# The bias of the values: one load and GpSimd adds instead of an accumulating DMA, in a two-layer graph network kernel

## The reference

```python
def setup_inputs(...):      # x is 4096 x 512, adj 4096 x 4096, sparse and symmetric, biases are small
...
def _L0_gnn_ref(x, spatial_encoding, edge_encoding, Wq, bq, Wk, bk, Wv, bv):
    q = x @ Wq.T + bq
    k = x @ Wk.T + bk
    v = x @ Wv.T + bv
    scale = 1.0 / jnp.sqrt(jnp.asarray(q.shape[-1], q.dtype))
    a = q @ k.T * scale + spatial_encoding + edge_encoding
    attn = jax.nn.softmax(a, axis=-1)
    return attn @ v
...
# --- layer 0 (adj_resnorm) ---
x = _layernorm(x + _L0_gnn_ref(x, adj, adj, ...), axis=-1)
# --- layer 1 (adj_resnorm) ---
x = _layernorm(x + _L1_gnn_ref(x, adj, W, b, a_self, a_neigh), axis=-1)
```

## Time and profile before

| | us |
|---|---|
| median of 3 runs | 1680.17 (1675.47 to 1684.64) |
| the profiled execution | 1676.71 |
| its span in the profile | 1674.9 |
| TensorE (PE) busy | 1561.0, 93% |
| VectorE (DVE) busy | 1218.4, 73% |
| GpSimd (POOL) busy | 866.4, 52% |
| ScalarE (ACT) busy | 539.9, 32% |
| mean transfer rate | 241 GB/s |

### The profile page before, as it was taken

How to read it: one execution, slowest core, us unless ns; L and a number is a source line. 1 busy time by engine, 2 the same in 40 slices (tenths; PEclk the granted TensorE clock), 3 DMA queues, 4 the chain that set the end, 5 groups by cost and what they waited for, 6 DMA issues and landing times.

```text
span 1674.9 us, 27914 instructions
## 1 busy us (share of the span) xinstructions
PE 1561.0 (93%) x10052; PEld 969.0 (58%) x10052; DVE 1218.4 (73%) x2438; ACT 539.9 (32%) x822; POOL 866.4 (52%) x809
## 2 busy tenths in 40 slices
PE   8999998999999999999999999999999999989830
PEld 3444587666666666666666666666666666644310
DVE  5798687688867876688768876887587867847335
ACT  4555401222232223222322233223322232246336
POOL 2987401556454644454545554555455545667343
PEclk9999999999999999999999999999999999999975
DMA  7467886679757886798669866896589667756347
GB/s 263 164 239 274 300 295 215 226 245 282 264 183 250 297 278 189 231 305 264 205 214 318 282 212 199 298 288 229 186 275 324 228 191 241 235 200 221 89 141 292
DMA packets 192396, 403.24 MB, mean 241 GB/s; under 512 B 20736, under 2 KB 26880, under 8 KB 191104
## 3 DMA queue, kind: packets, MB, share of 16 engines
q1 hardware_dynamic: 182912, 376.25, 67.0%
q0 software_dynamic: 9344, 25.17, 5.8%
HBM read 343.67 MB, written 57.67 MB: 240 GB/s over the span
## 4 chain that ended last, share of the span: by engine, by line
PE 83%; DVE 6%; DMA 4%; issue 2%; POOL 2%; ACT 1%; SPq 1%; another core or an unknown queue 0%; DVEq 0%; POOLq 0%; ACTq 0%
PE O L845 34%; PE S L804 30%; PE O L759 6%; PE X L759 5%; DMA yb<-y_scratch 3%; PE S L759 3%; PE O L804 2%; PE BC L759 1%; PE X L888 1%; POOL work L719 1%; DVE work L1362 1%; DVE ring L1601 1%; POOL ring L741 1%; DVE xr L1388 1%; DVE ring L1404 1%
## 5 line engine op out<-in xcount | busy, mean ns | idle before, releaser
L845 PE MATMUL O<-vring,ring 128*128 128x512 f16 x2928 | 707.5, 379 | 5.2 <-POOL ring L709 3.4
L804 PE MATMUL S<-yb,big 128*128 128x256 f16 x4974 | 621.3, 273 | 15.1 <-DMA yb<-y_scratch 6.9
L709 POOL TENSOR_TENSOR ring<-work,ring 128x512 f16<-128x512 f32 x236 | 282.6, 1198 | 599.5 <-ACT ring L1020 599.5
L804 PEld LDWEIGHTS S<-yb,big 128*128 128x128 f16 x4974 | 483.0, 98 | 167.4 <-issue 10.4
L845 PEld LDWEIGHTS O<-vring,ring 128*128 128x128 f16 x2928 | 286.1, 98 | 262.3 <-issue 7.4
L1141 ACT ACTIVATE work<-ring 128x512 f32<-128x512 f32 x256 | 160.8, 628 | 750.5 <-DVE ring L1327 705.9
L1336 DVE TENSOR_TENSOR ring<-S,ring 128x256 f32<-128x256 f32 x476 | 199.6, 419 | 219.6 <-PE S L804 216.9
L719 POOL TENSOR_TENSOR work<-work 128x512 f32<-128x512 f32 x248 | 342.9, 1383 | 7.0 <-ACT work L1141 5.9
L1362 DVE TENSOR_TENSOR work<-work,ring 128x512 f32<-128x512 f32 x248 | 207.4, 836 | 0.6
L1341 DVE TENSOR_TENSOR ring<-S,ring 128x256 f32<-128x256 f32 x357 | 150.6, 422 | 62.8 <-PE S L804 47.5
L1327 DVE TENSOR_TENSOR ring<-BC,ring 128x512 f32<-128x512 f32 x256 | 173.6, 679 | 1.8 <-PE BC L873 1.8
(11 more groups left out here) (145 smaller groups left out, 1096.3 us busy)
## 6 DMA issues: line engine op xcount, KB each, us to landing
ring<-in_adjT SPq DMA_DIRECT2D x256, 256.0 KB, 5.0
big<-in_adj SPq DMA_DIRECT2D x256, 256.0 KB
big<-x_scratch SPq DMA_DIRECT2D x126, 512.0 KB, 5.2
vring<-v_scratch SPq DMA_DIRECT2D x244, 256.0 KB
yb<-y_scratch SPq DMA_DIRECT2D x56, 256.0 KB, 6.2
y_scratch<-yb SPq DMA_DIRECT2D x7, 1792.0 KB, 10.6
ring<-in_xT SPq DMA_DIRECT2D x8, 1024.0 KB, 6.7
v_scratch<-vring SPq DMA_DIRECT2D x32, 256.0 KB, 2.6
```

Source lines behind the costliest of these rows:

```text
L709: pool.tensor_tensor(ring16[:, e % SLOTS, 1, :], pf[:, e % NPF, :], ring16[:, e % SLOTS, 0, :], ALU.subtract).then_inc(lo_done, 1)
L804: mm = pe.matmul(bank, keys_of(p, keys, a, c), yb[:, b % 2, queries, m, c, :], start=(start and c + a + m == 0), stop=(c == 1 and a == 1), ...
L845: mm = pe.matmul(O[j][:, :], ring16[:, e % SLOTS, a, j * P:(j + 1) * P], values_of(e)[:, m, :], start=(k + a + m == 0), stop=(k == NT - 1 ...
```

## The change

bv is loaded once a block by SP, as a fifth load behind the four of x, into `bvb`, which is the place of `x1h`. GpSimd adds it to the four tiles of `xr` with four instructions, two at r = 13 and two at r = 14, where it started one DMA before. The eviction of tile j waits for j + 1 of these adds.

```diff
+        bvb = work[:, 2560:3072]
...
-        xr_in, xb_in = sem("xr_in"), sem("xb_in")
+        xr_in, xb_set = sem("xr_in"), sem("xb_set")
...
                         sp.dma_start(xr[:, j, :], x[t * P:(t + 1) * P, :]).then_inc(xr_in, 16)
+                    sp.dma_start(bvb, row_of(bv)).then_inc(xr_in, 16)
...
-                if r == 13 and 1 <= b <= NB:
-
-                    pool.wait_ge(xr_in, b * JB * 16)
-                    pool.dma_start(xr[:, :, :], bv.rearrange("(a o n) -> a o n", a=1, o=1).broadcast_to([P, JB, D]),
-                                   accum_op=ALU.add).then_inc(xb_in, 16)
+                if r in (13, 14) and 1 <= b <= NB:
+
+                    pool.wait_ge(xr_in, b * (JB + 1) * 16)
+                    for j in (0, 1) if r == 13 else (2, 3):
+                        pool.tensor_tensor(xr[:, j, :], xr[:, j, :], bvb, ALU.add).then_inc(xb_set, 1)
...
-                dve.wait_ge(xb_in, (b + 1) * 16)
+                dve.wait_ge(xb_set, b * JB + j + 1)
```

## The result

The changed kernel takes 1695.07 us in the median of 5 runs (1691.64 to 1697.75), against 1680.17 before. The ratio is 1.0099, with a 95% interval of 1.0074 to 1.0123: slower by 1.0%. The forecast was 1676.7 us, the range 1670 to 1687. It was wrong, and on the other side.

What follows compares the result with a forecast made beforehand. TensorE, busy 1561.0 of 1674.9 us, was taken as the bound, losing time at block turns. -7.5 (DMA) + 0.7 (adds against VectorE) + 3.3 (tail) = -3.5 us, so 1676.7 us against the median 1680.2; range 1670 to 1687.

Steps and rivals of the forecast that it cites:

- The accumulating DMA: Turns between blocks: removing it frees DMA capacity, so the last piece of queries lands in time; -7.5 us.
- Rival 1: Turns between blocks: the queries stay late and only 1.7 us comes back; +2.3 us in all, 1682.5 us; chance 0.13.
- GpSimd's own time: Mid-kernel, r = 13 and 14: slack and idle time cover the adds; 0, or 25 us without that cover.
- the fifth load in mid-kernel: SP at r = 11: it moves the loads behind it by about 0.5 us, on chunks that aren't late; 0.
- the wait before the eviction: VectorE at r = 1 of the next block: it asks for xb_set some 30 us later; 0.
- So an add can hold a maximum back by up to 0.92 us: Mid-kernel, 28 adds against VectorE's running maximum: between 0 and 26 us, taken as 0.1 us a block, 0.7 us.
- the reads that TensorE waits for stand in front of the maximum: Mid-kernel, VectorE: why a maximum of 1.50 us delayed TensorE by nothing, its step still taking 9.76 us.
- Rival 2: Mid-kernel, r = 13 and 14: adds hold VectorE back, 11.2 us in place of 0.7; +7.0 us, 1687.2 us; chance 0.14.
- The tail: Last block, x loads to row sums: later landing and adds delay the running sums; +3.3 us, bounds 2.1 to 6.2.
- the fifth load adds one issue, 0.44 us: Tail: the load of bv lengthens GpSimd's wait for the last block's x rows by one issue, 1.75/4 = 0.44 us.
- The adds, 1.16 + 2.54 - 0.8 = 2.9 us: Tail: two adds replace the 1.38 us command, two more come two sums later, and 0.8 us is taken back.
- rival 3: Tail: after a longer gap TensorE's 36 products run at a lower clock, costing 3.4 us; -0.1 in all, 1680.1 us; chance 0.15.

Runs made afterwards that it cites:

- load_only: The changed kernel with bv loaded but not added, so the output lacks the bias; ratio 0.9960 to the kernel before.
- one_by_one: The changed kernel with one add behind each running sum of r = 13 and 14, not two behind the second; ratio 1.0014 to the kernel before.
- self_wait: The changed kernel, where GpSimd waits for each add of its own before its next instruction; ratio 1.0011 to the kernel before.
- no_gather: The changed kernel with the gather behind the adds of r = 13, and a wait and three very small GpSimd instructions in front; 1694.45 us, one execution.
- wait_second: The changed kernel, where GpSimd waits only for the second add of each pair; ratio 1.0026 to the kernel before.
- before_early: The kernel before with only the last block's four loads of x issued at r = 9, not r = 11; ratio 0.9967 to the kernel before.
- self_late: self_wait in seven blocks; the last block's four adds stand behind the last running sum, with bv loaded into mx; 1668.25 us, ratio 0.9925 to the kernel before.

## Why the prediction was wrong

**The accumulating DMA (predicted -7.5): right.** The mid-kernel of load_only is 7.3 us shorter in its trace; the waits at the turns are gone; the pieces of queries land in 7.9 us at most there and in 7.5 in the full change (predicted 6.4 to 7.5). Rival 1 is out. Its 1.7 us is 7.5 less the 5.8 of waits; the turn's own 0.44 us, five times, would have been 2.2.

**GpSimd's own time (0), the fifth load in mid-kernel (0), the wait before the eviction (0): right as far as the runs can tell.** one_by_one and self_wait carry all adds and reach the loads of x at 1540.69 and 1540.25, not later than load_only's 1542.42. Both traces are of quick executions, though, 2.7 and 5.8 us below the medians. By the ratios the two kernels lie 9.1 and 8.6 us above load_only, and their tails explain 6.7 and 7.3 of that; up to some 2 us could be the adds' own cost in mid-kernel, which is inside the intervals. Before its evictions VectorE waits for nothing but TensorE.

**"So an add can hold a maximum back by up to 0.92 us" (predicted +0.7): this step failed.** It measured 14.9 us, inside the bound of 26, and in another way than the bound said. The 0.92 us was read from the earlier trace rows, where a maximum meets a remainder and a sum and gets in at the next end of an instruction. With add, add, remainder and sum in one unbroken row it waited for all of them, 4.0 to 4.6 us over its 0.68. The second half of the step failed with it: "the reads that TensorE waits for stand in front of the maximum" held for a maximum of 1.50 us, but one of 5.25 us reaches past the next step's reads. Four such meetings, not 28 small delays, made 11.7 us of waits and 3.4 us of lower clock. The Trainium skill (SBUF — State Buffer, "Who interferes with whom") has the second engine blocked until the first has finished. The traces agree that these two engines hold each other up, and go beyond the page in the length: a wait of 4.0 us or more did not end with the instruction of 1.2 us that it met.

Rival 2 named the side and the place, with 11.2 us against the 14.9 measured, and I gave it 0.14. Its argument against itself was one step with one maximum of 1.50 us. I had also bounded the idle time of GpSimd for the remainder's sake only. The order of GpSimd's instructions, a wait-free row of four where a DMA command had parted them, was on record and not read as a term.

**The tail (predicted +3.3, bounds 2.1 to 6.2): mis-sized, measured +9.7.** Up to the row sums, which is what the sum counted, it is +6.1, at the upper bound; 3.6 us come behind them. The term "the fifth load adds one issue, 0.44 us" measured 2.2 us: GpSimd waits for the load of bv, which lands 6.5 us after its issue at 1559.09, and not only for one issue more. Over the traces with the loads at r = 11, this wait ends 7.3 to 8.3 us after the first issue with five loads, and 5.3 and 6.1 us with four. In load_only the removed command and quicker sums pay for it: its row sums come 17.1 us after the loads, as before. The adds, 1.16 + 2.54 - 0.8 = 2.9 us, measured 3.8. The 0.8 us came back: the six sums take 2.67 + 6.61 = 9.3 us where they took 10.05. But the four adds took 5.4 us and not 5.08, since two of them met a VectorE remainder (L1407) and took 2.94; and the command that they replaced had held the sums up by 0.9 us (1555.77 to 1556.66 in the earlier trace rows), not by its whole 1.38. The rest is rival 3, which came true beside the others and not in their place, at 3.6 us where it was priced at 3.4: row sums of 1.71 us and 36 products of 10.86 us in place of 7.93, at a granted clock of 0.50 to 0.71. It fell within TensorE's idle time of 10.19 us: in windows of 1 us it is 1.00 until 1567, some 5 us behind the last product, and 0.50 from 1568 on. In the kernel before it likewise fell within the idle time of 5.87 us, at 0.50 from 1558 on, and not only behind it; it was back at 1.00 by 1565 us, while TensorE still had three products at a time; here it stayed low through all of these and through some 6 us of the 36 products.

**The sum.** -7.3 + 14.9 + 9.7 + 1.2 = 18.5 us between the profiled executions, 18.4 measured; the 1.2 is the spread of the last stretch. The medians differ by 14.9 us, since the profiled execution of before lies 3.5 us below its median and that of the change on it. With the meetings avoided (self_wait) the sum by the same marks is -9.5 + 7.3, and the ratio 1.0011: the forecast's sign of the mid-kernel holds and the tail takes it back.

**Open.** Why VectorE gets in between two GpSimd instructions without a pause in some meetings and not in others. It often does between a remainder and a sum (as in the row of 1.50 us in the earlier trace rows) and did at 579.57 us in no_gather between two adds; it didn't in the six long ones, nor between the adds in wait_second, nor between remainder and sum behind the gather at 406.68 and 1103.52 us in no_gather. A wait of GpSimd for its own instruction let it in each time that was looked at. Also open is why the clock fell after two of the four waits: they were 3.48 and 2.51 us, and those of 3.21 and 2.51 us left it at 1.00. And open is the spread of 6 us in the stretch behind the second eviction.

## What to carry to other kernels

Before GpSimd gets one more full-width instruction in SBUF, write down the unbroken row that it makes with its neighbours, and price a meeting with a two-operand VectorE instruction at up to the length of that row, not of one instruction; then see what VectorE owes TensorE behind it. If the row must stay, a wait of GpSimd for its own last instruction broke it here, for a gap of 0.08 us and what the next instruction then pays (0.35 us). An addition that only an epilogue needs belongs behind the last instruction on which the end hangs, and its load counts as landing time there, not as one more issue.

## What the runs showed of the hardware

- A VectorE instruction of 0.68 us took 5.26 us beside GpSimd instructions of 1.2 us each that ran without a pause, and 1.72 us when GpSimd waited for its own add first. Without such a wait the row was not always waited out: once VectorE got in between two adds (1.42 us).
- A load of one row of 2 KB into 128 partitions (256 KB) landed 6.5 us after its issue in the tail. GpSimd's wait ended 8.3 us after the first issue with it, and 6.1 us with the four tiles of 256 KB alone.
- An idle time of TensorE of 2.5 to 3.5 us in mid-kernel left the granted clock at 1.00 twice and was followed by a stretch at 0.52 or 0.53 twice; in the tail it fell within an idle time of 10.19 us and was at 0.50 from 1570 to 1585 us, first with three products at a time and then with full work. Where the same groups of three came with no longer idle time than 0.9 us (before_early, self_late), it stayed at 1.00.
